# Attention with split-bf16 matmuls: the next head pair's K and V are made between the steps of the current one

## What is computed

```python
def attn(query, Wq, Wk, Wv, Wp, bp):
    q = jnp.einsum('bnd,hde->bhne', query, Wq) * scale
    k = jnp.einsum('bmd,hde->bhme', query, Wk)
    v = jnp.einsum('bmd,hde->bhme', query, Wv)
    attn = jax.nn.softmax(jnp.einsum('bhne,bhme->bhnm', q, k), axis=-1)
    out = jnp.einsum('bhnm,bhme->bnhe', attn, v)
    out = jnp.swapaxes(out, -1, -2).reshape(B, N, E * H)
    return jnp.dot(out, Wp) + bp

x = x + attn(layernorm(x), ...)
x = x + experts(layernorm(x), ...)     # 8 dense experts, gated, threshold 0.1
```

## Time and profile before

| | us |
|---|---|
| median of the runs | 8316.83 (7802.9 to 8344.91, 3 runs) |
| the profiled execution | 7802.9 |
| its span, slowest core (3) | 7801.3 |
| spans of the 8 cores | 7787.3 to 7801.3 |
| mean granted PE clock, each core | 0.873 to 0.875 |
| busy: PE, DVE, ACT, POOL | 5736.2, 3636.0, 2315.5, 882.7 |

### The profile page before, as it was taken

One profiled execution on the slowest core, in us unless ns is written; L12 is line 12 of the kernel. 1 busy time (PEld: TensorE's weight loads), 2 busy tenths in 40 slices (PEclk: granted clock), 3 DMA queues, 4 the chain that ended last, 5 costly groups with the idle time before them and its releaser, 6 DMA issues.

```text
span 7801.3 us, 85281 instructions; the slowest of 8 cores (7787.3 to 7801.3 us)
## 1 busy us (share of the span) xinstructions
PE 5736.2 (74%) x24598; PEld 2530.2 (32%) x24598; DVE 3636.0 (47%) x6022; ACT 2315.5 (30%) x3501; POOL 882.7 (11%) x1028
## 2 busy tenths in 40 slices
PE   3548777786876786876776886777236457999999
PEld 1223333333333333333333333333012223444444
DVE  4235565555555565555555555556433333112111
ACT  1114443443443443443443443444011111000000
POOL 0001111211111121111121211112000000000000
PEclk8769988998998998998998998999568667999999
DMA  1111111111111111111121111111011000000001
GB/s 47 54 46 29 31 32 33 31 29 37 29 31 34 32 28 35 29 31 35 31 33 33 31 28 36 29 32 25 1 38 46 4 0 22 33 22 22 33 22 44
DMA packets 259072, 237.54 MB, mean 30 GB/s; under 512 B 32173, under 2 KB 196143, under 8 KB 258616
## 3 DMA queue, kind: packets, MB, share of 16 engines
q0 software_dynamic: 57344, 68.22, 7.6%
q1 hardware_dynamic: 201272, 163.87, 6.7%
HBM read 155.33 MB, written 8.39 MB: 21 GB/s over the span
## 4 chain that ended last, share of the span: by engine, by line
PE 49%; DVE 26%; ACT 9%; issue 7%; DVEq 5%; ACTq 3%; DMA 2%; SPq 0%
PE psW L181 12%; PE psW L182 11%; PE psW L183 11%; DVE ptl L498 9%; DVE pth L495 7%; DVEq L906 4%; ACTq L906 2%; ACT stg L513 2%; PE psT L181 2%; PE psT L182 2%; PE psT L183 2%; ACT ptf L487 2%; PE psPVa L181 1%; DVE rdbuf L602 1%; DVE wvl L175 1%
## 5 line engine op out<-in xcount | busy, mean ns | idle before, releaser
L487 ACT ACTIVATE ptf<-psW,cns 128x512 f32<-128x512 f32 x2048 | 1407.7, 687 | 1184.6 <-PE psW L183 759.6
L498 DVE TENSOR_TENSOR ptl<-ptf,pth 128x512 bf16<-128x512 f32 x2048 | 1416.5, 692 | 157.9 <-issue 5.5
L495 DVE CAST pth<-ptf 128x512 bf16<-128x512 f32 x2048 | 874.5, 427 | 459.1 <-ACT ptf L487 274.6
L181 PE MATMUL psW<-q_h,k_h 128*128 128x512 bf16 x2048 | 777.2, 380 | 0.0
L183 PE MATMUL psW<-q_h,k_l 128*128 128x512 bf16 x2048 | 777.2, 379 | 0.0
L182 PE MATMUL psW<-q_l,k_h 128*128 128x512 bf16 x2048 | 776.8, 379 | 0.0
L523 POOL DMA_DIRECT2D big<-stg x256 | 229.5, 897 | 4570.6 <-ACT stg L513 3760.8
L181 PE MATMUL psPVa<-pth,vah 128*65 128x512 bf16 x1024 | 387.6, 379 | 320.2 <-ACT stg L513 177.3
L181 PE MATMUL psW<-weh,ln2h 128*128 128x512 bf16 x1408 | 546.6, 388 | 20.8 <-DVE out_acc L764 15.2
L182 PE MATMUL psW<-wel,ln2h 128*128 128x512 bf16 x1408 | 545.5, 387 | 0.0
L183 PE MATMUL psW<-weh,ln2l 128*128 128x512 bf16 x1408 | 545.1, 387 | 0.0
(11 more groups left out here) (137 smaller groups left out, 7537.3 us busy)
## 6 DMA issues: line engine op xcount, KB each, us to landing
big<-stg POOLq DMA_DIRECT2D x512, 128.0 KB, 3.4
xst<-xin SPq DMA_DIRECT2D x64, 512.0 KB, 3.6
wstg<-wk SPq DMA_DIRECT2D x64, 512.0 KB
wstg<-wv SPq DMA_DIRECT2D x64, 512.0 KB, 4.4
estg<-we SPq DMA_DIRECT2D x16, 2048.0 KB, 9.0
wstg<-wq SPq DMA_DIRECT2D x32, 512.0 KB, 3.4
den<-stg POOLq DMA_DIRECT2D x512, 2.0 KB, 3.4
y<-out_acc SPq DMA_DIRECT2D x32, 256.0 KB, 2.0
```

The lines of the kernel that those rows point to most:

```text
L181: p.op("T", lambda e: e.matmul(out_ap, lh, rh, start=start, stop=False))
L487: e.activation(ptf[gpar][:, :], pss[:, off:off + QB], AF.Exp, bias=cns[:, 0:1], scale=0.125))
L495: e.tensor_copy(pth[s][par][:, :], ptf[gpar][:, :]))
L498: e.tensor_tensor(ptl[s][par][:, :], ptf[gpar][:, :], pth[s][par][:, :], ALU.subtract))
```

## The change

K and V tiles exist twice (`kh2`, `kl2`, `vah2`, `val2`, a set for odd and one for even units). `make_gen_cbs` returns the making of K and V of a unit as ten pieces. The first unit of a window runs them at once, as before; in every other case the pieces for the next unit are put between the steps of the current one, one after each of the steps 2, 5, 8, ..., 29. Both projections now go into the two halves of `psW[2]` (psT), which the transposes use too. What runs in a piece is the same as before: same loads, splits, matmuls, transposes.

`den` shrinks from 128 x 2048 to 128 x 256 floats; each head's 512 denominators of a query block lie in two rows of 256 instead of in one row. `den` and `rdbuf` are allocated at the right side of SBUF. The waits that guard K and V (`kread_free`) name the last PV of the unit before the current one. The number of `memset`s at the start grows by eight.

```diff
-        den = sb("den", [128, QH])
...
+                HB = QB // 2
+                den = esab.enter_context(
+                    nc.sbuf_tensor("den", [128, HB], F32, side="right"))
...
-                k_h = [sba("k_h%d" % s, [128, MB], BF16) for s in range(2)]
+                kh2 = [[sba("kh%d%d" % (g, s), [128, MB], BF16)
+                        for s in range(2)] for g in range(2)]
...
+                def make_gen_cbs(mb, pi, seti, lnev):
+                    st = {}
+                    kh, kl = kh2[seti], kl2[seti]
+                    vah, val = vah2[seti], val2[seti]
+
+                    def cb_kload():
+                        st["wkev"] = load_w_slice(wk, pi, 0)
+
+                    def cb_kcvt():
+                        _, st["wkevl"] = cvt(wkh[:, :], wkl[:, :], wstg[:, :],
+                                             DC * 128, st["wkev"])
+                        wstg_free[0] = st["wkevl"]
+
+                    def cb_kgen():
+                        st["evk"] = gen_mm(psW[2], wkh, wkl, st["wkevl"],
+                                           lnev, base=0)
+
+                    def cb_kevac():
+                        p.waits("A", kread_free[seti])
+                        p.waits("V", kread_free[seti])
+                        _, ev1 = cvt(kh[0][0:64, :], kl[0][0:64, :],
+                                     psW[2][0:64, 0:MB], MB, st["evk"])
+                        _, evkl = cvt(kh[1][64:128, :], kl[1][64:128, :],
+                                      psW[2][64:128, 0:MB], MB, st["evk"])
+                        ps_read(psW[2], evkl, (0,))
+                        evkl_set[seti] = evkl
...
+                    def cb_vgen():
+                        st["evv"] = gen_mm(psW[2], wvh, wvl, st["wvevl"],
+                                           lnev, base=512)
+
+                    def cb_vevac():
+                        p.wait("A", st["evv"])
+                        p.op("A", lambda e: e.copy(vstg[:, :],
+                                                   psW[2][:, 512:512 + MB]))
...
+                    return [cb_kload, cb_kcvt, cb_kgen, cb_kevac,
+                            cb_vload, cb_vcvt, cb_vgen, cb_vevac,
+                            mk_vtrans(0), mk_vtrans(1)]
+
+                units = [(mb, pi) for mb in range(NB) for pi in range(NP)]
+                lnev_cur = None
+                for ui, (mb, pi) in enumerate(units):
+                    seti = ui % 2
+                    if pi == 0:
+                        lnev_cur = ln_window(mb * MB, MB // 128)
+                        for cb in make_gen_cbs(mb, 0, seti, lnev_cur):
+                            cb()
...
+                    if pi + 1 < NP:
+                        gen_cbs = make_gen_cbs(mb, pi + 1, (ui + 1) % 2,
+                                               lnev_cur)
+                    else:
+                        gen_cbs = []
...
+                        p.op("G", lambda e, pi=pi, qb=qb, sg=sg: e.dma_start(
+                            bass.AP(den, (pi * NQB + qb) * 2 * HB,
+                                    [[HB, 2], [1, HB]]),
+                            stage[sg][64:65, 0:QB], accum_op=ALU.add))
...
+                    for i, st2 in enumerate(steps):
+                        ch_ev, par = emit_S_chain(i, *st2)
+                        pend.append((st2, ch_ev, par))
+                        if len(pend) > 3:
                             emit_PV(*pend.pop(0))
+                        if gen_cbs and i >= 2 and (i - 2) % 3 == 0:
+                            gen_cbs.pop(0)()
+                    while gen_cbs:
+                        gen_cbs.pop(0)()
+                    while pend:
+                        emit_PV(*pend.pop(0))
+                    kread_free[seti] = [p.now(chT)]
```

More of the change, by code:

```diff
@@ L296, in build_program @@
                 stage = [sba("stg%d" % i, [128, 2 * QB]) for i in range(2)]
-                rdbuf = sba("rdbuf", [128, QB])
+                rdbuf = esab.enter_context(
+                    nc.sbuf_tensor("rdbuf", [128, QB], F32, side="right"))
                 lnsc = sba("lnsc_ab", [128, D])
[L300 to L307, removed]
+                for g in range(2):
+                    for s in range(2):
+                        p.op("V", lambda e, g=g, s=s: e.memset(
+                            vah2[g][s][:, :], 1.0))
+                        p.op("V", lambda e, g=g, s=s: e.memset(
+                            val2[g][s][:, :], 0.0))
+                        rows0 = slice(64, 128) if s == 0 else slice(0, 64)
+                        p.op("V", lambda e, g=g, s=s, rows0=rows0: e.memset(
+                            kh2[g][s][rows0, :], 0.0))
+                        p.op("V", lambda e, g=g, s=s, rows0=rows0: e.memset(
+                            kl2[g][s][rows0, :], 0.0))
                 ev_va_init = p.inc(chV)
-                va_free = [[ev_va_init], [ev_va_init]]
                 xst_free = [None, None]
@@ L399, in build_program @@
                 q_ready = p.now(chV)
-                k_free = []
-                v_free = []
                 pair_acc_ev = [[None, None] for _ in range(NP)]
[L404 to L436, removed]
@@ L437, in build_program @@
                             off = s * 512
-                            ps_wait("T", pst, (s,))
-                            p.wait("T", evvs)
-                            p.waits("T", va_free[s])
+                            ps_wait("T", psW[2], (s,))
+                            p.wait("T", st["evvs"])
+                            p.waits("T", psT_tr_free[s])
                             for c in range(MC):
-                                p.op("T", lambda e, s=s, c=c, pst=pst, off=off:
+                                p.op("T", lambda e, s=s, c=c, off=off:
@@ L443, in build_program @@
                                      e.transpose(
-                                         pst[:, off + c * 64:off + (c + 1) * 64],
+                                         psW[2][:, off + c * 64:
+                                                off + (c + 1) * 64],
                                          vstg[s * 64:(s + 1) * 64,
@@ L457, in build_program @@
                             _, eva = cvt(hiap, loap,
-                                         pst[:, off:off + MC * 64],
+                                         psW[2][:, off:off + MC * 64],
                                          MC * 64, evt)
[L460 to L504, removed]
@@ L545, in emit_PV @@
[L545 to L548, removed]
-                            p.wait("T", chain_ev)
-                            p.wait("T", ev_va[s])
-                            mm3(psPV[s][0:65, 0:QB],
-                                vah[s][:, c * VS:c * VS + 65],
-                                val[s][:, c * VS:c * VS + 65],
-                                pth[s][par][:, :],
-                                ptl[s][par][:, :],
-                                start=(c == 0), stop=(c == MC - 1))
-                            ev_pv = p.inc(chT)
-                            pthl_free[s][par] = ev_pv
-                            if c == MC - 1:
-                                pv_done[s] = ev_pv
-                                if s == 1:
-                                    flush_qb(qb)
@@ L564, in build_program @@
-                        steps = [(qb, c, s) for qb in range(NQB)
-                                 for c in range(MC) for s in range(2)]
-                        pend = []
-                        for i, st in enumerate(steps):
-                            ch_ev, par = emit_S_chain(i, *st)
-                            pend.append((st, ch_ev, par))
-                            if len(pend) > 3:
-                                emit_PV(*pend.pop(0))
-                        while pend:
-                            emit_PV(*pend.pop(0))
@@ L586, in build_program @@
                             rdrep[0:1, 0:QB],
-                            den[pi:pi + 1, qb * QB:(qb + 1) * QB]))
+                            bass.AP(den, (pi * NQB + qb) * 2 * HB,
+                                    [[HB, 2], [1, HB]])))
                         p.inc(chC)
@@ L590, in build_program @@
                             rdrep[1:2, 0:QB],
-                            den[pi + NP:pi + NP + 1, qb * QB:(qb + 1) * QB]))
+                            bass.AP(den, ((pi + NP) * NQB + qb) * 2 * HB,
+                                    [[HB, 2], [1, HB]])))
                         evd = p.inc(chC)
```

185 lines of the change are left out of this document (133 added, 52 removed).

## The result

| | us |
|---|---|
| before, median | 8231.07 (7802.54 to 8481.26, 14 runs) |
| changed kernel, median | 7623.67 (7256.39 to 7906.41, 14 runs) |
| ratio, executions within 1.5% of the best | 0.9335, 95% interval 0.928 to 0.9391 |

The account below looks back on a forecast made before the run. PE was busiest but unsaturated, alternating with other engines and tied with DVE within steps. 52.1 us PE work plus 8.3 stalls gave 60.4 a unit against 71.5; 56 units save 622, so 7802.9 becomes 7180 us, range 7040 to 7450.

Parts of the forecast that it names:

- the 2.14 us stall left the clock at 1.00: Argument that stalls inside attention's steps would not lower PE's clock, since the longest one seen, 2.14 us, had not.
- (d): PE stall at the flush after PV(15), with V's weight cast after step 17: 2.6 us a unit.
- a rival in which a whole phase runs at the low clock: Stalls inside attention's steps drop PE's clock; at 0.70 throughout, 82.7 us a unit, 8430 us; chance 0.03.
- (a): PE stall at the start of a unit, where the first PV waits behind stage copies and exp: 1.2 us.
- (b): PE stall where K's matmuls wait for K's weight cast, put in after step 5: 0.7 us a unit.
- (c): K's 24 matmuls after step 8, then the ordinary flush stall after PV(7): 1.3 us a unit.
- (e): ACT copy after step 23 costs nothing; third flush, into which the first transposes fall, stalls PE 1.3 us.
- (f): Second transposes after step 29 put 0.5 us on DVE, so the unit's end stall grows from 0.65 to 1.2 us.
- transposes: PE time of the 8 small transposes in a unit, taken as 0.4 us in all.
- DVE as the bound: Rival: the projections absorb none of DVE's 5.2 us extra work; 64.0 us a unit, 7383 us; chance 0.12.
- the clock does not rise with the denser work: Rival: attention keeps its mean granted clock of 0.90; 66.2 us a unit, 7506 us; chance 0.08, including down to 0.82.
- the 7850 us estimated with it: Estimate under the skill's 13/16 clock limit: 72.4 us a unit, kernel about 7850 us, no change.

Follow-up runs that it names:

- e6: e5 with K's weights for the unit after next loaded and cast directly behind V's matmuls, in all units and across windows; 6933.7 us.
- e5: Changed kernel with K's 24 matmuls directly behind PV(7) and V's 24 directly behind PV(15), casts and K's evacuation moved to suit; 6984.7 us.
- e3: Changed kernel with V's weight cast moved from behind step 17 to right behind K's 24 matmuls (behind step 8); 7154.7 us.
- run 800: Not a follow-up run: "run" is a verb here, all 8 cores execute 800 us of the experts at granted clock 1.00.

## Why the prediction was right and wrong

**The time.** The sum was made from the profiled execution of 7802.9 us and given as the forecast, although the prediction itself noted a median 514 us above it. This step failed first: the measured median is 368 us above the best execution of the changed kernel. Against that execution 7180 was 76 us too low, inside the range, and 547 of 622 us were gained.

**Where the 76 us went.** The period of a unit was forecast as 60.4 and measured as 61.5 us: 1.1 x 56 = 62 us. Another 14 us stand in the last unit of each window: a window takes 545.9 us in the mean, and 545.9 - 7 x 61.53 = 115.2 us for that unit with LayerNorm and first projections, where 23.5 + 48.0 + 42 = 113.5 were counted, 8 x 1.7 us. Behind its first flush (2.13 us) the clock falls in 7 of the 8 windows, 1.7 us each. 5 us are no part of attention: on the profiled core it begins at 578 us instead of 571, and the part behind it takes 2351 instead of 2353 us. Some 6 us go the other way: a unit of the kernel before takes 71.6 us in the mean, not 71.5.

**The clock inside the units.** The step that failed is "the 2.14 us stall left the clock at 1.00", read from one unit and carried over to a stall of 2.6 us. The trace of the kernel before had the answer elsewhere: of its 60 stalls of 2.1 to 2.3 us, two are followed by slow intervals. The PE timeline of one of them, at the start of a unit:

```profile
2440.07 0.38 PE L183 MATMUL psW<-q_h,k_l 128*128 128x512 bf16 x1
2442.48 0.38 PE L181 MATMUL psPVa<-pth,vah 128*65 128x512 bf16 x1 [2.03 <-DVE ptl L498]
...
2443.57 0.63 PE L183 MATMUL psW<-q_h,k_l 128*128 128x512 bf16 x1
2443.99 0.63 PE L181 MATMUL psPVb<-pth,vah 128*65 128x512 bf16 x1
```

The prediction named the place, behind (d), but as a rival in which a whole phase runs at the low clock, with a chance of 0.03. The fall happens there and lasts for about 3.6 us. V's early cast shortens the stall and takes nearly all falls away (3 left of 44), and the forecast of that run (2.4 us a unit) was 0.6 us too high, mostly because 12 of 56 units had had no fall.

**The stalls.**

| | forecast | measured |
|---|---|---|
| (a) start of unit | 1.2 | 1.25 |
| (b) K's cast | 0.7 | 0.6 |
| (c) first flush | 1.3 | 1.3 |
| (d) second flush | 2.6 | 2.5 |
| (e) third flush | 1.3 | 0.8 |
| (f) end of unit | 1.2 | 0.6 |
| transposes | 0.4 | 1.0 |
| clock | 0 | 1.7, in most units |

(a) to (d) were right in size. The runs bear out (b) (e6 takes the cast away and gains), (c) and (d) (e5 fills both flushes) and the 0.6 us of the cast in (d) (e3); the working of (a) was not tested. In (e) the stall is shorter by the 0.5 us that four transposes take in PE's queue, which the text said but the sum did not subtract. In (f) the stall stayed the 0.65 us of before: DVE's extra subtract cost nothing. The transposes come as two groups of four, each 0.5 us, where 0.4 us for all eight was read from a row of eight in one. The errors in (e), (f) and the transposes cancel to 0.5 us; without the clock the forecast would have been 0.4 us a unit too high.

**Where costs of nothing were right.** den's layout (0.3 us), the loads (no wait of a weight cast on a DMA; landing in 3.5 to 5.3 us), the second set of tiles (nothing). DVE as the bound is out: it is busy 40.5 of 61.6 us, and with better places the unit went down to 56.0 us.

**The clock of a whole die.** The rival "the clock does not rise with the denser work" was put aside because the end of the profiled execution before was granted 1.00. One execution does not speak for all. In 10 of the 14 executions of the changed kernel the cores of one die have a mean granted clock of 0.78 to 0.89 and the longest spans, while those of the other keep 0.89 and 7229 to 7260 us; in three more both dies are granted less. In that of 7727.42 us the clock records hold a third value beside 0.5 and 1.00, 0.8125, for 4139 of 7726 us on the profiled core, and a unit under it takes 68.2 us (the row in the first section). This is the step that put the measured median outside the range. Its price was off too. The prediction says that the gain is gone at a granted clock of 0.82, but it held the kernel before at its best time, and that one is longer in such executions as well: between the medians the gain is 607 us. And by its own formula the stalls of that unit are 68.2 - 52.1 / 0.8125 = 4.1 us and not 8.3: they shrink where PE is slower. The Trainium skill, "TensorE: Matmul & The Clock Gate", Part 1, names a limit of 13/16 for a die with dense matmuls on three or more cores. With this the trace agrees in that row, and disagrees in the executions of 7803 and 7256 us, where all 8 cores run 800 us of the experts, PE busy 774 us or more, at 1.00; the 7850 us estimated with it was too high, since not every stretch had that clock and the stalls were smaller.

## What to carry to other kernels

When work of another kind is woven into a pipelined loop, put it where the engine that sets the pace waits for something else: the same 48 matmuls gave 547 us between evenly spaced steps and 271 us more when they lay in the flush waits. Price each insertion in the queue of every engine it touches, and count how long the in-order queues stand behind a piece whose input is late: weaving LayerNorm in was to give 210 us and gave 28, and 59 with one step more. Count a rare event over all repeats in the trace, not in one, and say whether a forecast is for the profiled execution or for the median.

## What was not expected of the hardware

A short stall of a busy PE can lower its clock for about 3.6 us. Counted behind the stalls at the start of a query block, on the profiled core: of up to 2.1 us none in all the kernels without LayerNorm woven in; of 2.1 to 2.3 us 2 of 60 in the kernel before, but 7 of 8 in the last units of the changed kernel's windows, where the stall and the steps of the unit ahead of it are the same (over all eight cores 6 of 481 and 52 of 64); of 2.5 us and more 44 of 56; of 3.2 us 39 of 56. So length alone does not decide. What came before may matter: ahead of these steps the kernel before has its projections, granted 0.78, and the changed kernel the dense steps of another unit. The place matters as well: behind a stall that is 2.54 us in the median in both, the clock falls in 60 of 64 cases in the second unit of a window and in 33 of 64 in the fourth (eight windows, eight cores). The runs don't tell why.

The time that all 8 cores are granted the full clock is not the same in every execution of one kernel: 7256 to 7906 us in 14 executions of the changed one.
